# Mamba, attention and MoE decoder on one core: one product for B and C, the router's steps and the two streams' self-attention steps in another order, attention outputs copied by ScalarE

## The chip, the cores and the metric

The kernel runs on one core of a Trainium2 chip (trn2). The metric is the device time of one execution in microseconds (us); lower is better. Times are the median of 3 runs; the profile is of one more execution.

## What is computed

Eight sequences (batches) of 256 tokens, 256 channels, all in float32, pass through two layers. After every block stands a layer norm of input plus block.

```python
# layer 0: mamba without recurrence
xc    = silu(conv4(x @ W_in[:512].T));  z = x @ W_in[512:].T
proj  = xc @ W_xproj.T                       # 16 columns B, 16 columns C, 512 columns delta
bc    = (proj[..., :16] * proj[..., 16:32]).sum(-1)
x     = ln(x + ((softplus(proj[..., 32:]) * xc * bc[..., None] + D * xc) * silu(z)) @ W_out.T)
x     = ln(x + cross_attention(x, ctx_768))  # 16 heads of 64, 77 keys
# mixture: shared expert of 1024, and 2 of 8 routed experts of 256
scores = sigmoid(x @ router_w.T);  top2(scores + expert_bias)
x     = ln(x + shared(x) + routed(x, gates))
# layer 1
x     = ln(x + self_attention(x))            # 16 heads of 16, rotary embedding
x     = ln(x + cross_attention(x, ctx_768))
# last block: every token attends to the tokens of its own class (similarity over or under 0.9)
x     = ln(x + masked_attention(x))          # 16 heads of 16
```

## The kernel before

**Streams.** Even batches belong to stream 0, odd ones to stream 1. Each stream has four PSUM banks of its own (2048 float32 columns, the tile names `ps0` and `ps1`) and rooms of its own in SBUF (`m30` and `m31` are the two streams' large rooms in layer 1, `r..` the rooms for split operands, `sm..` small ones). Every product of float32 data outside the attentions is made of three matmuls on split operands (L114, L115, L116). Transposes are L644, and a plain copy by ScalarE is L1188.

**Order of the work.** Every engine works through its instructions in order. For each stage and engine the program holds the list of steps of stream 0 and that of stream 1, and a table of numbers (FIRST for layer 0, SECOND for self attention, cross attention and the projections of the last block in layer 1, LAST for the masked attention) says after how many steps of stream 0 the next step of stream 1 is issued:

```python
for j in range(4 * n):
    want = n * (j // n) + after[j % n]
    while done < want:
        next(first, None)
        done += 1
    next(second, None)
```

**Stages.** Layer 0 for all batches; then the router's scores (transposed, `rt`), gates and choice; the shared expert in four units of 256 hidden columns, two halves each, in which the streams take turns (`moe`); the indices of the tokens' places among the experts (`slots`), scatters by GpSimd with these indices, 23 routed tiles of 256 tokens, gathers back; then layer 1 for four pairs of batches, and the masked attention for four pairs.

**Router and shared expert.** DVE makes the gates of two groups of four token tiles, `gates((0, 1))`, before the shared expert and `gates((2, 3))` and `choose()` behind the first turn of stream 0. A turn of a half is: up products h1 and h2 on PE, ScalarE's silu, DVE's product (`L1509 ps<-m,ps 128x1024`) and split (`L1509 r<-ps,r`), then a turn later the down product and its sum to `xres` (`L1509 xres<-ps,xres x4`). The PE part of the indices (`slots_of`, L853 and L859) stands in stream 1's second turn, and `slots()`, one block of 27 DVE rows from L1739 to L1785, ahead of stream 1's first sum to `xres`.

**Self attention, masked attention.** A batch has four groups c of four heads. First come maxima: 16 matmuls of queries by keys fill all four banks of the stream (`mx`, L989), a DVE reduce takes the row maxima (`nm`, L1520 from 128x2048), and the next group follows. The maxima are transposed (`t2`) and added to the queries (`T2`). Then come rounds: scores with keys as rows into all four banks (`s`, L1008, 16 matmuls), Exp by ScalarE to the room (`e`, L1406, 128x2048), values times weights into bank c (`o`, L1014, 16 matmuls), and a copy of that bank's 256 columns to SBUF (`ot`, L1885 in `out_of`, by DVE), for which `s` of the next group waits. After the fourth come transposes (`t3`), the division, `oT` and the output projection `y`. In the trace a name like `m<-ps` is without stream numbers.

## Time and profile before

| | |
|---|---|
| median of 3 runs | 1649.91 us (1648.32 to 1650.14) |
| profiled execution, its own time | 1653.7 us |
| its span, first to last instruction | 1651.9 us |
| granted TensorE clock over the span | 0.921 of full |
| PE busy | 1408.8 us (85%), 12280 matmuls |
| DVE busy | 981.9 us (59%), 1739 instructions |
| ScalarE (ACT) busy | 635.9 us (38%), 743 instructions |
| GpSimd (POOL) busy | 420.0 us (25%), 434 instructions |

Stages by the trace: layer 0 to about 457 us; router and shared expert to about 640; routed experts to 769; layer 1 to 1355, a pair of batches each 143 us; the choice of classes to 1361; the masked attention to the end, a pair each 68 us.

How to read it: busy shares are over the whole span, and stages differ. A view in windows gives each engine's busy time and, as PEclk, the share of the full clock that TensorE was granted. A timeline row has start and duration in us, engine, line, operation, output<-inputs, shapes, a count, and in brackets how long the engine was idle before and who released it. A row of several matmuls (x16) is one run of them.

### The profile page before, as it was taken

How to read it: one execution, taken by the hardware profiler on the slowest of the kernel's cores; microseconds unless marked ns; L12 is line 12 of the kernel's file. 1: busy time of each engine (PE TensorE's matmuls, PEld its weight loads, DVE VectorE, ACT ScalarE, POOL GpSimd, SP SyncE). 2: the span in 40 equal slices, each digit the busy share in tenths (PEclk: the TensorE clock that was granted, in tenths of full speed). 3: DMA queues.
4: the chain of work that ended last, by engine and by line, in shares of the span. 5: the costliest groups of instructions: out<-in, count | busy, mean ns of one | idle time of the engine just before them, and what ended most of it. 6: DMA issues, size and time to landing. Idle time of an engine off the chain costs nothing.

```text
span 1651.9 us, 28489 instructions
## 1 busy us (share of the span) xinstructions
PE 1408.8 (85%) x12280; PEld 1149.8 (70%) x12280; DVE 981.9 (59%) x1739; ACT 635.9 (38%) x743; POOL 420.0 (25%) x434
## 2 busy tenths in 40 slices
PE   5899999999967999998699779969978957878785
PEld 5688888887846878997478548847855845556453
DVE  5676666756636445666745755675583555565663
ACT  3453344444522334662244244324424511422413
POOL 2230020210321653665113602622240340000000
PEclk8899999999978999998799999979999986977969
DMA  9100000000040222782000100100000020101000
GB/s 376 55 1 1 1 1 1 1 1 1 1 178 10 80 90 99 271 279 99 13 1 1 64 1 1 41 25 1 1 39 1 1 115 1 40 21 46 1 14 14
DMA packets 28495, 82.24 MB, mean 50 GB/s; under 512 B 3153, under 2 KB 13009, under 8 KB 27345
## 3 DMA queue, kind: packets, MB, share of 16 engines
q1 hardware_dynamic: 25296, 72.02, 12.1%
q0 software_dynamic: 3072, 8.39, 1.6%
q8 instruction: 97, 1.59, 0.4%
q14 instruction: 30, 0.24, 0.0%
HBM read 53.92 MB, written 26.48 MB: 49 GB/s over the span
## 4 chain that ended last, share of the span: by engine, by line
PE 33%; DVE 14%; ACT 3%; POOL 2%; issue 2%; DMA 0%; another core or an unknown queue 0%; POOLq 0%; DVEq 0%; ACTq 0%
DVE sm L1520 7%; PE ps L644 5%; PE ps L1008 4%; PE ps L1014 4%; PE ps L114 3%; PE ps L115 3%; PE ps L116 3%; PE ps L989 2%; PE ps L760 2%; PE ps L776 2%; PE ps L656 2%; PE ps L649 2%; DVE m L1509 2%; ACT m L1188 2%; DVE m L1885 1%
## 5 line engine op out<-in xcount | busy, mean ns | idle before, releaser
L1188 ACT ACTIVATE m<-ps 77x1024 f32<-77x1024 f32 (+4 forms) x248 | 183.8, 759 | 364.1 <-PE ps L116 156.8
L1520 DVE TENSOR_REDUCE sm<-ps 128x8 f32<-128x2048 f32 (+1 forms) x128 | 194.1, 1536 | 63.9 <-PE ps L989 43.6
L1509 DVE TENSOR_TENSOR r<-ps,r 128x512 fp32r<-128x512 f32 (+1 forms) x159 | 116.1, 741 | 157.0 <-ACT r L1188 157.0
L2113 POOL TENSOR_SCALAR sm<-sm 128x2 f32<-128x2 f32 x40 | 8.7, 218 | 761.9 <-DVE sm L1538 761.9
L1188 ACT ACTIVATE r<-ps 128x512 fp32r<-128x512 f32 (+1 forms) x159 | 100.7, 639 | 255.5 <-PE ps L644 120.5
L1406 ACT ACTIVATE m<-ps 128x2048 f32<-128x2048 f32 x64 | 119.3, 1877 | 154.1 <-PE ps L1008 154.1
L644 PE MATMUL ps<-cst,m 128*77 128x128 f32 (+2 forms) x1024 | 142.6, 282 | 26.7 <-DVE m L1509 6.5
L644 PEld LDWEIGHTS ps<-cst,m 128*77 128x77 f32 (+2 forms) x1024 | 117.0, 149 | 58.3 <-issue 18.0
L114 PE MATMUL ps<-r,w0h 128*128 128x256 f32 x448 | 133.0, 297 | 16.9 <-DVE r L1509 12.6
L989 PE MATMUL ps<-m 32*128 32x256 f32 x1024 | 102.5, 538 | 39.4 <-DVE sm L1520 24.0
L116 PE MATMUL ps<-r,w0l 128*128 128x256 f32 x448 | 129.8, 290 | 0.0
L115 PE MATMUL ps<-r,w0h 128*128 128x256 f32 x448 | 129.6, 289 | 0.0
L2142 POOL TENSOR_TENSOR m<-m,sm 128x616 f32<-128x616 f32 x64 | 76.7, 1216 | 147.2 <-DVE sm L1634 147.2
L989 PEld LDWEIGHTS ps<-m 32*128 32x128 f32 x1024 | 64.7, 258 | 69.1 <-DVE sm L1520 44.2
L1008 PE MATMUL ps<-m 32*128 32x256 f32 x1024 | 83.0, 448 | 31.2 <-DVE m L1885 28.7
L114 PEld LDWEIGHTS ps<-r,w0h 128*128 128x128 f32 x448 | 89.0, 199 | 19.4 <-DVE r L1509 14.7
L114 PE MATMUL ps<-w1h,r 128*128 128x256 f32 (+1 forms) x288 | 95.0, 330 | 6.3 <-DVE r L1509 6.3
L1008 PEld LDWEIGHTS ps<-m 32*128 32x128 f32 x1024 | 53.8, 211 | 61.5 <-DVE m L1885 51.1
L1885 DVE COPY m<-ps 128x256 f32<-128x256 f32 x64 | 27.0, 422 | 110.3 <-PE ps L1014 110.3
L1509 DVE TENSOR_TENSOR xres<-ps,xres 128x256 f32<-128x256 f32 (+1 forms) x104 | 50.2, 522 | 67.0 <-PE ps L116 63.7
L115 PEld LDWEIGHTS ps<-r,w0h 128*128 128x128 f32 x448 | 88.8, 198 | 1.0 <-issue 1.0
L115 PE MATMUL ps<-w1l,r 128*128 128x256 f32 (+1 forms) x288 | 89.3, 310 | 0.0
(241 smaller groups left out, 3621.1 us busy)
## 6 DMA issues: line engine op xcount, KB each, us to landing
raw<-wu_dram SPq DMA_DIRECT2D x20, 768.0 KB
keep_dram<-m SPq DMA_DIRECT2D x8, 768.0 KB, 3.2
m<-keep_dram SPq DMA_DIRECT2D x8, 768.0 KB, 4.4
xs_dram<-small SPq DMA_DIRECT2D x2, 2944.0 KB, 32.5
ys_dram<-m SPq DMA_DIRECT2D x23, 256.0 KB
room<-wu_dram SPq DMA_DIRECT2D x7, 768.0 KB, 4.7
rt<-xs_dram SPq DMA_DIRECT2D x16, 256.0 KB, 3.6
w1raw<-w_dram SPq DMA_DIRECT2D x1, 3840.0 KB, 14.4
```

What stands on the lines that cost most here:

```text
L114: pe.matmul(o, l[0], r[0], start=start, stop=False)
L115: pe.matmul(o, l[0], r[1], start=False, stop=False)
L116: return pe.matmul(o, l[1], r[0], start=False, stop=stop)
L644: return pe.transpose(o, i, ident[0:n, 0:n])
L989: m = pe.matmul(bank(st, a)[:, 256 * j:256 * j + 256], v.qT[r:r + 32, c, 128 * j:128 * j + 128], v.kT[r:r + 32, c, :], start=True, stop=True)
L1008: m = pe.matmul(bank(st, a)[:, 256 * k:256 * k + 256], v.kT[r:r + 32, c, 128 * k:128 * k + 128], v.qT[r:r + 32, c, :], start=True, stop=True)
L1014: m = pe.matmul(bank(st, c)[32 * a:32 * a + 32, 0:256], v.va[:, k, 4 * c + a, :], w[:, a, k, :], start=k == 0, stop=k == 1)
L1188: return act.activation(o, i, ACT.Copy)
L1406: act.activation(v.P, st.ps[:, :], ACT.Exp, scale=0.25).then_inc(sig.up(b, f"e{c}"), 1)
L1509: return dve.tensor_tensor(o, a, b_, op)
L1520: return dve.tensor_reduce(o, i, AX.X, op, **kw)
L2142: pool.tensor_tensor(pw, pw, v.rc[u].unsqueeze(2).to_broadcast([P, 8, CK]), ALU.mult).then_inc(sig.up(b, f"p{u}"), 1)
```

## The change

1. **B and C.** The weight W_xproj is laid out with 16 columns of zeros between B and C, so that one product of 48 columns gives B in PSUM rows 0 to 15 and C in rows 32 to 47. Before, two products of 128 columns each gave them in rows 0 to 15 of two column ranges. 12 matmuls in place of 24 per batch.
2. **Router, gates, indices.** The scores' transposes are issued in the middle of stream 0's first turn; all four groups of gates and the choice stand ahead of the shared expert's halves; `slots_of` is issued at the end of stream 1's first turn, in bank 1 of stream 0, and so waits for stream 0's silu; the wait for the copy `cp` stands on PE ahead of stream 0's first down product; the DVE block `slots()` is cut in three pieces with turns' work between them.
3. **Gathers and first norms.** Stream 1's first gather is issued one tile later; the first layer norms of layer 1 are issued between the last routed tiles.
4. **Copies `ot`.** In self attention and masked attention ScalarE copies the four outputs, 64 copies in all; DVE has none.
5. **Orders.** New tables SECOND and LAST for all engines. FIRST is unchanged.

The diff, cut:

```diff
-LAY0 = [("win", 1024), ("wz", 1024), ("wxp", 2176), ("wout", 1024), ("wq", 2048), ("wo", 2048)]
+LAY0 = [("win", 1024), ("wz", 1024), ("wxp", 2240), ("wout", 1024), ("wq", 2048), ("wo", 2048)]
...
 SECOND = {
-    "PE": [1, 2, 4, 5, 5, 6, 7, 8, 9, 10, 12, 12, 14, 14, 16, 16, 18, 19, 25, 26, 26, 26, 27, 31, 34, 35, 38, 38, 38, 41, 42, 46, 46, 48, 50, 51, 52, 52, 53, 54, 54, 54, 54, 55, 55, 56, 56, 56, 56, 56, 56, 56, 57, 57, 57, 57, 58, 60, 60],
+    "PE": [3, 5, 7, 8, 9, 10, 12, 13, 14, 15, 16, 17, 18, 19, 21, 23, 24, 25, 26, 26, 26, 26, 31, 31, 33, 35, 38, 39, 41, 43, 43, 45, 45, 47, 51, 51, 54, 56, 56, 56, 56, 56, 57, 57, 59, 59, 59, 59, 59, 60, 60, 60, 60, 60, 60, 60, 61, 61, 61],
...
+        EXPOT = [f"{w}{c}" for c in G4 for w in ("e", "ot")]
-        A1ACT = ["xT", "va", "Tk", "Tq", *EXP, "oT"]
-        A1DVE = ["xT", "c", "a0", "t0", "a1", "t1", *NM, "T2", *[f"ot{c}" for c in G4], "rc", "on", "oT", *LN]
+        A1ACT = ["xT", "va", "Tk", "Tq", *EXPOT, "oT"]
+        A1DVE = ["xT", "c", "a0", "t0", "a1", "t1", *NM, "T2", "rc", "on", "oT", *LN]
...
-                        mm3(pe, st.ps[:, 1024 + c * 256:1280 + c * 256], cols(v.wxp, A, k, slice(32 + c * 128, 160 + c * 128)), cols(v.xr, A, k), k == 0, k == 3)
-                yield
-                for c in range(2):
-                    for k in range(4):
-                        m = mm3(pe, st.ps[:, c * 256:(c + 1) * 256], cols(v.wxp, A, k, slice(16 * c, 16 * c + 128)), cols(v.xr, A, k), k == 0, k == 3)
+                        mm3(pe, st.ps[:, 1024 + c * 256:1280 + c * 256], cols(v.wxp, A, k, slice(48 + c * 128, 176 + c * 128)), cols(v.xr, A, k), k == 0, k == 3)
+                yield
+                for k in range(4):
+                    m = mm3(pe, st.ps[0:48, 0:256], cols(v.wxp, A, k, slice(0, 48)), cols(v.xr, A, k), k == 0, k == 3)
...
-                o = bank(streams[1], 3)
+                o = bank(streams[0], 1)
                 og = o[:, 0:128].rearrange("p (g i e) -> p g i e", g=4, i=4)
                 cg = chosen.rearrange("p (g i e) -> p g i e", g=4, i=4)
+                pe.wait_ge(*streams[0].moe_act.at(*MOE[0], "silu"))
                 pe.wait_ge(*gate_dve.at("four"))
...
                 for turn, (n, k) in enumerate(MOE):
                     half = st.i + 2 * k
+                    if turn == 1 and st.i == 0:
+                        pe.wait_ge(*gate_dve.at("cp"))
                     if prev is not None:
                         down(st, *prev)
-                    if turn == 1 and st.i == 1:
-                        slots_of()
                     a, b_ = turn % 2, 1 - turn % 2
                     up = tuple(k2(w[:, 0:1024]) for w in uw[n % 2])
...
-                        elif c == 1 and turn == 1 and st.i == 1:
-                            pe.wait_ge(*gate_dve.at("cp"))
                         elif c >= 2 and turn == 0:
                             pe.wait_ge(*gate_act.at("th", 2 * st.i + c % 2))
+                            if c == 2 and st.i == 0:
+                                turn_scores()
                             if c == 3 and st.i == 1:
...
-                    if turn == 0 and st.i == 0:
-                        turn_scores()
+                    if turn == 0 and st.i == 1:
+                        slots_of()
...
-                    pe.wait_ge(*dve_.at(b, f"ot{c - 1}" if c else "T2"))
+                    pe.wait_ge(*(act_.at(b, f"ot{c - 1}") if c else dve_.at(b, "T2")))
...
-                copy(v.Bc[0:16, :], st.ps[0:16, 0:256]).then_inc(sig.up(b, "B"), 1)
+                copy(v.Bc[0:16, :], st.ps[32:48, 0:256]).then_inc(sig.up(b, "B"), 1)
...
+                    yield
+                    act.wait_ge(*pe_.at(b, f"o{c}"))
+                    copy(v.OT[:, c, :], bank(st, c)[:, 0:256]).then_inc(sig.up(b, f"ot{c}"), 1)
...
-                tt(v.Bc[0:16, :], v.Bc[0:16, :], st.ps[0:16, 256:512], ALU.mult).then_inc(sig.up(b, "Bc"), 1)
+                tt(v.Bc[0:16, :], v.Bc[0:16, :], st.ps[0:16, 0:256], ALU.mult).then_inc(sig.up(b, "Bc"), 1)
...
-                dve.tensor_copy(counts, bank(streams[1], 3)[:, 0:136]).then_inc(sig.up("cp"), 1)
+                dve.tensor_copy(counts, bank(streams[0], 1)[:, 0:136]).then_inc(sig.up("cp"), 1)
+                yield
...
-                    if turn == 1 and st.i == 1:
-                        slots()
                     if turn:
                         down(st, turn - 1)
+                    if turn == 1:
+                        next(finding, None)
...
-                        gates((2, 3))
-                        choose()
-                    yield
-
-            gates((0, 1))
+                        next(finding)
+                    yield
+
+            gates(range(4))
+            choose()
+            finding = slots()
...
+            firsts = [norm_only(st, st.batches[0]) for st in streams]
...
                     routed_add(streams[0], 0)
+                    next(firsts[0])
                 elif j == NT - 2:
+                    next(firsts[0])
+                    next(firsts[0])
                     routed_add(streams[1], 1)
-            together([norm_only(st, st.batches[0]) for st in streams])
+                    next(firsts[1])
+            for first in firsts:
+                for _ in first:
+                    pass
...
-            def out_of(st, b, v, sig, pe_, c):
-                dve.wait_ge(*pe_.at(b, f"o{c}"))
-                dve.tensor_copy(v.OT[:, c, :], bank(st, c)[:, 0:256]).then_inc(sig.up(b, f"ot{c}"), 1)
...
-                elif j == NT - 3:
+                elif j == NT - 2:
                     gather(streams[1], 1)
...
+    wxp = a["L0_attn_W_xproj"].T
+    wxp = np.concatenate([wxp[:, 0:16], np.zeros((512, 16), np.float32), wxp[:, 16:]], 1)
```

**How instructions move on PE, self attention of batches 2 and 3.** Here `L989`/`L990` are maxima, `L1008`/`L1009` scores, `L1014`/`L1015` values by weights (lines before and after), `L644`/`L645` with `sm` the transposed maxima `t2`; `ps0<-m30` belongs to stream 0 and `ps1<-m31` to stream 1. Before:

```order
L989 MATMUL ps1<-m31 128x256 x8
L989 MATMUL ps0<-m30 128x256 x8
L989 MATMUL ps1<-m31 128x256 x8
L644 MATMUL ps0<-cst,sm0 128x128 x2
L644 MATMUL ps1<-cst,sm1 128x128 x2
L1008 MATMUL ps0<-m30 128x256 x8
L1008 MATMUL ps1<-m31 128x256 x8
L1014 MATMUL ps0<-m30 32x256 x8
L1008 MATMUL ps0<-m30 128x256 x8
L1014 MATMUL ps1<-m31 32x256 x8
L1008 MATMUL ps1<-m31 128x256 x8
```

Now:

```order
L645 MATMUL ps0<-cst,sm0 128x128 x2
L990 MATMUL ps1<-m31 128x256 x8
L1009 MATMUL ps0<-m30 128x256 x8
L990 MATMUL ps1<-m31 128x256 x8
L1015 MATMUL ps0<-m30 32x256 x8
L1009 MATMUL ps0<-m30 128x256 x8
L990 MATMUL ps1<-m31 128x256 x8
L1015 MATMUL ps0<-m30 32x256 x8
L990 MATMUL ps1<-m31 128x256 x8
L1009 MATMUL ps0<-m30 128x256 x8
L645 MATMUL ps1<-cst,sm1 128x128 x2
L1015 MATMUL ps0<-m30 32x256 x8
```

Before, the two streams take turns at maxima and then at rounds; now stream 1's maxima stand between stream 0's rounds, and its own rounds begin when stream 0's end.

**How instructions move on ScalarE, the same place.** `L1406`/`L1407` are the Exp, `L1188`/`L1189` copies. Before:

```order
L1188 ACTIVATE m31<-ps1 128x1024 x2
L1406 ACTIVATE m30<-ps0 128x2048
L1406 ACTIVATE m31<-ps1 128x2048
L1406 ACTIVATE m30<-ps0 128x2048
L1406 ACTIVATE m31<-ps1 128x2048
L1406 ACTIVATE m30<-ps0 128x2048
```

Now:

```order
L1407 ACTIVATE m30<-ps0 128x2048
L1189 ACTIVATE m30<-ps0 128x256
L1407 ACTIVATE m30<-ps0 128x2048
L1189 ACTIVATE m30<-ps0 128x256
L1407 ACTIVATE m30<-ps0 128x2048
L1189 ACTIVATE m30<-ps0 128x256
L1407 ACTIVATE m31<-ps1 128x2048
L1407 ACTIVATE m30<-ps0 128x2048
L1189 ACTIVATE m31<-ps1 128x256
L1189 ACTIVATE m30<-ps0 128x256
L1407 ACTIVATE m31<-ps1 128x2048
L1189 ACTIVATE m31<-ps1 128x256
```

Each Exp of a stream is followed by the 128x256 copy of its output; only at the handover from stream 0 to stream 1 does stream 0's last Exp stand between the first Exp and the first copy of stream 1.

**How instructions move on DVE, shared expert, first turns.** `ps0<-m20,ps0` and `r20` are stream 0's product and split, `ps1`, `r21` those of stream 1, `xres<-ps0` the sum of stream 0's down product, `L1739`/`L1743` the copy `cp` with which `slots()` begins. Before:

```order
L1520 TENSOR_REDUCE rt<-rt 128x32
L1509 TENSOR_TENSOR ps1<-m21,ps1 128x1024
L1509 TENSOR_TENSOR r21<-ps1,r21 128x1024
L1509 TENSOR_TENSOR xres<-ps0,xres 128x256 x4
L1509 TENSOR_TENSOR ps0<-m20,ps0 128x1024
L1509 TENSOR_TENSOR r20<-ps0,r20 128x1024
L1739 COPY rt<-ps1 128x136
```

Now:

```order
L1524 TENSOR_REDUCE rt<-rt 128x32
L1513 TENSOR_TENSOR ps0<-m20,ps0 128x1024
L1513 TENSOR_TENSOR r20<-ps0,r20 128x1024
L1743 COPY rt<-ps0 128x136
L1513 TENSOR_TENSOR ps1<-m21,ps1 128x1024
L1513 TENSOR_TENSOR r21<-ps1,r21 128x1024
L1513 TENSOR_TENSOR xres<-ps0,xres 128x256 x4
L1513 TENSOR_TENSOR rt<-rt,cst 128x64
```

The choice (the reduce of 32) now ends ahead of stream 0's first product and not between the two streams' first products, and the copy `cp` comes a turn earlier.

## Rows read from the trace of the kernel before

**Rows 1.** The page: granted clock of TensorE in 40 slices, tenths.

```profile
PEclk8899999999978999998799999979999986977969
```

**Rows 2.** Windows: layer 0, MoE start, maxima, rounds, cross attention, masked attention.

```profile
core 0: us, PE busy (x) PEld busy (x) DVE busy (x) ACT busy (x) POOL busy (x), PEclk, DMA share, GB/s
130.00:400.00 270.00, 251.70 (x1899) 222.64 (x1898) 175.58 (x343) 119.71 (x137) 34.06 (x44) 0.98 0.00 1
500.00:540.00 40.00, 29.81 (x154) 25.48 (x153) 24.37 (x64) 7.06 (x7) 6.89 (x7) 0.87 0.06 20
...
1078.65:1098.00 19.35, 12.46 (x124) 8.01 (x128) 17.83 (x9) 0.00 (x0) 3.29 (x4) 0.73 0.09 28
1098.00:1124.50 26.50, 20.50 (x260) 10.98 (x252) 10.62 (x31) 14.91 (x8) 2.10 (x4) 0.88 0.01 2
1124.50:1183.00 58.50, 57.43 (x428) 48.42 (x428) 33.15 (x58) 26.80 (x40) 16.43 (x18) 1.00 0.00 1
1380.00:1652.00 272.00, 210.11 (x3057) 140.24 (x3055) 157.14 (x277) 83.84 (x82) 7.45 (x16) 0.82 0.06 21
```

**Rows 3.** Chain of waits: first maxima of two pairs, layer 1 and last.

```profile
935.40 1.19 PE ps L989 x16
...
1078.65 1.19 PE ps L989 x16
...
1511.40 2.09 PE ps L989 x16
...
1579.36 2.09 PE ps L989 x16
```

**Rows 4.** Timeline of PE, start of a pair's projections and its next stage.

```profile
1050.23 0.40 PE L114 MATMUL ps<-w1h,r 128*128 128x512 f32 x1
...
1134.73 0.60 PE L644 MATMUL ps<-cst,xres 128*128 128x128 f32 x4
```

**Rows 5.** Groups by form, one pair of layer 1, 935.40 to 1078.65.

```profile
L1520 DVE TENSOR_REDUCE sm<-ps 128x8 f32<-128x2048 f32 x8 | 18.0, 2288 | 4.7 <-PE ps L989 3.0 <-remote 1.7
```

**Rows 6.** Timeline, a half round of each stream.

```profile
965.33 1.15 PE L1008 MATMUL ps<-m 32*128 32x256 f32 x16 [0.55 <-DVE m L1885]
...
966.40 1.07 PE L1014 MATMUL ps<-m 128*32 128x256 f32 x16
966.54 1.88 ACT L1406 ACTIVATE m<-ps 128x2048 f32<-128x2048 f32 x1 [0.82 <-PE ps L1008]
967.54 0.42 DVE L1885 COPY m<-ps 128x256 f32<-128x256 f32 x1 [2.27 <-PE ps L1014]
...
968.02 1.15 PE L1008 MATMUL ps<-m 32*128 32x256 f32 x16 [0.55 <-DVE m L1885]
```

**Rows 7.** Timeline of PE at the end of layer 0.

```profile
453.40 0.28 PE L114 MATMUL ps<-w0h,r 128*128 128x256 f32 x1
...
453.76 0.28 PE L114 MATMUL ps<-w0h,r 128*128 128x256 f32 x1
```

**Rows 8.** Timeline of PE, shared expert, where it waited.

```profile
505.65 0.39 PE L114 MATMUL ps<-uw,r 128*128 128x256 f32 x1 [2.58 <-DVE r L1509]
...
515.06 0.50 PE L114 MATMUL ps<-xTall,uw 128*128 128x512 f32 x1 [2.02 <-DVE xres L1509]
...
531.77 0.80 PE L114 MATMUL ps<-xTall,uw 128*128 128x512 f32 x1 [5.58 <-DVE xres L1509]
```

**Rows 9.** Timelines of DVE and POOL: first and last index step, last scatter.

```profile
523.38 0.30 DVE L1739 COPY rt<-ps 128x136 f32<-128x136 f32 x1 [1.68 <-PE ps L859]
...
530.22 0.18 DVE L1785 CAST sm<-sm 128x32 uint32<-128x32 f32 x1
...
600.14 0.96 POOL L2186 DMA_INDIRECT xs_dram<-w1f,sm  x1 [0.30 <-issue]
```

**Rows 10.** Groups by form, 400 to 1652 us: ScalarE's copies from PSUM.

```profile
L1188 ACT ACTIVATE m<-ps 128x1024 f32<-128x1024 f32 x44 | 44.0, 1021 | 62.1 <-PE ps L116 41.4 <-PE ps L644 16.4 <-issue 4.2
...
L1188 ACT ACTIVATE m<-ps 128x512 f32<-128x512 f32 x48 | 26.9, 600 | 90.7 <-PE ps L644 45.0 <-PE ps L116 40.9 <-POOL m L2261 4.7
```

More of the change, by code:

```diff
@@ L291, in ffn_dve @@
                 o += [(b, s) for s in ("nx0", "nx", "x2", *NM, "T2")]
-                o += [nxt[0], (b, "ot0"), nxt[1], (b, "ot1"), nxt[2], (b, "ot2"), nxt[3], nxt[4]]
-                o += [(b, s) for s in ("ot3", "xr", "xn", "xc", "rc", "on", "ov", "oT", *LN)]
+                o += nxt
+                o += [(b, s) for s in ("xr", "xn", "xc", "rc", "on", "ov", "oT", *LN)]
             return [s for s in o if s is not None]
@@ L311, in ffn_act @@
                     o += [(b, s) for s in ("Tqa", "Tk", "Tq", "xe")]
-                o += [(b, s) for s in ("ex", "xo", *EXP)]
+                o += [(b, s) for s in ("ex", "xo", *EXPOT)]
                 nxt = [(b + 2, s) for s in ("Tqa", "Tk", "Tq", "xe")] if b + 2 < B else []
@@ L1064, in a1 @@
                 yield
-                pe.wait_ge(*dve_.at(b, "ot3"))
+                pe.wait_ge(*act_.at(b, "ot3"))
                 turn_out(st, b, v, sig)
@@ L1143, in fa @@
                 yield
-                pe.wait_ge(*dve_.at(b, "ot3"))
+                pe.wait_ge(*act_.at(b, "ot3"))
                 turn_out(st, b, v, sig)
@@ L1935, in a1 @@
                 yield
-                for c in range(4):
-                    yield
-                    out_of(st, b, v, sig, pe_, c)
                 yield
@@ L2066, in fa @@
                 nxt = front(st, b + 2) if b + 2 < B else iter(())
-                for c in range(4):
+                for c in range(5):
                     next(nxt, None)
-                    yield
-                    out_of(st, b, v, sig, pe_, c)
                     yield
@@ L2224, in norm_only @@
                 yield
-            together([norm_only(st, st.batches[0]) for st in streams])
+            for st in streams:
+                for _ in norm_only(st, st.batches[0]):
+                    pass
             last_moe(pool)
@@ L2356, in kv @@
         return np.concatenate([wk[0:P], wv[0:P], np.concatenate([wk[P:CD], wv[P:CD]], 0)], 1)
+    wxp = a["L0_attn_W_xproj"].T
+    wxp = np.concatenate([wxp[:, 0:16], np.zeros((512, 16), np.float32), wxp[:, 16:]], 1)
     conv = np.concatenate([a["L0_attn_conv_w"], a["L0_attn_conv_b"][:, None], a["L0_attn_D"][:, None]], 1)
-    w0 = np.concatenate([rows(a["L0_attn_W_in"][:512].T), rows(a["L0_attn_W_in"][512:].T), rows(a["L0_attn_W_xproj"].T), rows(a["L0_attn_W_out"].T),
+    w0 = np.concatenate([rows(a["L0_attn_W_in"][:512].T), rows(a["L0_attn_W_in"][512:].T), rows(wxp), rows(a["L0_attn_W_out"].T),
                          rows(a["L0_xattn_Wq"]), rows(a["L0_xattn_Wo"])], 1)
```

12 lines of the change are left out of this document (6 added, 6 removed).

## The prediction

> **What bounds the kernel now.** I read the page first, then the chain of waits for the stages, then the stages in windows, then timelines where the change touches them. Granted clock by slice [rows 1] is full or nearly full in layer 0 and around the middle, and lowest (6 to 7 tenths) in slices of the masked attention. The windows [rows 2] show two kinds of stage. In layer 0 PE is busy 251.7 of 270 us, in layer 1's cross attention 57.43 of 58.5: there only fewer matmuls help. In the self attention no engine is full. With the maxima DVE is the bound, 17.83 of 19.35 us, and PE, 12.46, is granted 0.73 of its clock. In the rounds PE has 20.50 of 26.5, ScalarE 14.91, DVE 10.62, and the masked attention is alike: PE 210 of 272 us at 0.82. So the stages that the new tables touch are bound by handoffs, and the two phases have opposite bounds. A pair of batches takes 1078.65 - 935.40 = 143.25 us in layer 1 and 1579.36 - 1511.40 = 67.96 in the masked attention [rows 3]. I cost the change part by part; it has five parts with a price.
>
> **B and C.** Three split matmuls of 256 columns take 453.76 - 453.40 = 0.36 us [rows 7], 0.12 each; 12 fewer per batch are 1.43, in eight batches 11.4 us. PE works 93% of the stage [rows 2], so nearly all of it lies on the path; but the products stand in a stretch where DVE's conv and ScalarE's steps of the same batch follow one another, and I take 85%: **9.7** (bounds 7 and 11.4). The copy from rows 32 to 47 is the same ScalarE instruction. I cost a product of 48 output rows as one of 128, since no row shows one of 48.
>
> **Router, gates, indices.** PE waits 2.58, 2.02 and 5.58 us before three products [rows 8]: for the split behind the second pair of gate groups, for a sum behind it, and for stream 1's sum, which stands behind the whole index block, 523.38 to 530.40 on DVE [rows 9]. In the change all gates stand ahead of the first product while PE has the halves' products to do, and the block is in three pieces under products. Laid out by hand with the rows' durations: the choice is done at about 504.0 (509.6 before), stream 0's first down product starts at 507.7, the counts at 518, the last index at 524.7, and the product that stood at 540.30 starts at 527.5. That is 12.8 less: about 10.2 of gaps become 2.8 (the new waits: the first product for its two DVE steps, the down product for `cp`), and 3 to 5 come from products that ran slow behind the gaps; the window from 500 to 540 had 0.87 of the clock [rows 2]. Behind PE's new wait for `cp` stands all of PE's stream 0; DVE reaches `cp` 0.3 us behind the split, so it costs little. I take **12** (bounds 5.7, the index time alone, and 13). Scatters start 5.7 earlier; the last was at 600.14 [rows 9], and the first routed tile is some 40 us behind it, so GpSimd's queue is no bound either way.
>
> **Gathers and first norms.** One gather a tile later, norms ahead of the last tile's output: **1** (0 to 3); DVE had the norms to do directly behind.
>
> **Self attention.** From the first projection of a pair to the transposes ahead of its cross attention the trace has 1134.73 - 1050.23 = 84.5 us [rows 4]. In it lie 8 maxima at 2.29 on DVE, 18.3 us [rows 5], and 8 half rounds at 968.02 - 965.33 = 2.69, 21.5 us [rows 6]: both streams pay for each other's steps, 39.8 together. In the new order a stream goes alone: a maximum is 1.19 of PE [rows 3] plus 0.1 plus 2.29, so 3.58, four are 14.3. A round is 1.21 from `s` to the Exp, 1.88 of Exp, 0.05, 1.14 from `o` to its copy [rows 6], the copy and 0.06. ScalarE's copies from PSUM take 1.02 us at 1024 columns and 0.60 at 512 [rows 10], by a straight line 0.39 at 256, against DVE's 0.42 [rows 6]; so a round is 4.73, take 4.8, four 19.2. Stream 1's maxima stand beside stream 0's rounds (DVE is free there), its rounds beside what stream 0 does next. With all steps laid out (only stream 0's projection and rotary steps now stand ahead of the first maximum) 84.5 becomes 76.5, **8.0** less. Given back: the next pair's gathers and norms now meet the division on DVE, 1.6, and stream 1's last transposes stand ahead of stream 0's cross attention, 1.0; 5.4 stay. The clock takes more: stream 1's rounds, alone, keep PE busy 2.2 of 4.8 us, less than the 12.46 of 19.35 that ran at 0.73 [rows 2]. A group of 16 matmuls is 1.19 at the full level and 2.09 at the half level [rows 3], 0.90 more; five such groups on the path are 4.5, and 0.9 would stay. The maxima before were at 0.73 as well and now run beside other products, so I take the middle, 3.5 a pair; four pairs less 1 at the end, where stream 1 is late: **13** (2.6 to 20.6). The move of the copies alone is worth nothing here, 0.03 us each.
>
> The row says ScalarE has room, 14.91 of 26.5, but DVE with 10.62 has more [rows 2]. The Trainium skill (Perfetto Trace Analysis, Optimizing Scalar/DVE Operations) says that work should go from DVE to ScalarE if DVE is saturated. By that rule part 4 brings nothing, and without the orders' gain the sum would end near 1627; what I count comes from the orders, which let DVE do maxima in the rounds: without its four copies (1.7) and with four maxima (9.2) it would be some 18 of 26 us busy there.
>
> **Masked attention.** The same 39.8 become 14.3 + 19.2 = 33.5, 6.3 less of 67.96, and 0.7 more since DVE's projections for the next pair no longer wait between copies: 61.0 a pair at equal clock. Here the clock was low before, 0.82 over the stage [rows 2], and `L989` at 2.09 [rows 3]; four more slow groups, 3.6, would leave about 3. I take 5, three periods, less 1.3 at the end: **13.7** (7.7 to 19.7).
>
> **Sum.** 9.7 + 12 + 1 + 13 + 13.7 = 49.4. The profiled execution took 1653.7 (span 1651.9); that gives 1604.3, and against the median of 1649.91, which lies 3.8 below it, 1600.5. Forecast **1601**. All lower bounds together give 23, so 1627; all upper ones 68, so 1582.
>
> **Rivals.**
> - *The clock.* If TensorE is at its 1.2 GHz level in all of a lone stream's rounds, eight groups at 0.90 are 7.2 a pair: layer 1 loses 1.8 a pair and 7 in all, the masked attention gains nothing. 9.7 + 12 + 1 - 7 - 1 = 14.7: about 1635. For it: 0.73 and 0.82 in sparse stretches [rows 2]. Against it: in the half rounds before, PE was 77% busy and `L1008` at full speed [rows 6], and stream 0's rounds now have maxima beside them. The Trainium skill (TensorE: Matmul & The Clock Gate, A second HAM failure mode) tells of a kernel whose short idles between groups made the clock swing between the levels, which speaks for this rival; the trace agrees in that 1.19 and 2.09 both occur for the same 16 matmuls. Chance 0.15.
> - *Only the index time.* If the slow products behind the gaps stay slow, the MoE term is 5.7: 1607, and 1611 if the routed stage waits for POOL. Against it: no gap of over 2.6 us is left in my layout. Chance 0.08; inside the range.
> - *Copies behind the other stream's Exp: slower.* ScalarE works in order. If a stream's copy regularly stands behind the other's Exp, `s` waits for it: a half step is then 1.88 + 0.39 + 0.06 + 1.22 = 3.55 in place of 2.69, 0.86 for each of 64 copies, 55 us, and the attention gains are lost too: 1649.9 - 22.7 + 55 = 1682. It decides from 22.7 / 0.86 = 26 of 64 copies on. For it: the Exps of both streams did follow each other in the old order. Against it: in the new order of ScalarE one copy of eight per pair of layer 1 (stream 1's first) stands behind the other stream's Exp, and none in the masked attention. Chance 0.07.
> - *Nothing comes of it,* as the gains are all taken back by later waits: 1650. Both the PE-bound layer 0 and the gaps speak against it. Chance 0.03.
> - *More,* near 1580: the clock rises as maxima and rounds fill one another's gaps. Chance 0.05.
>
> **How the numbers follow.** The forecast case has 0.62. A difference of 0.2%, 3.3 us, is about what a measurement of this kernel can tell from no change. Faster by more: 0.62 + 0.15 + 0.08 + 0.05 = 0.90; same 0.03; slower 0.07. The range 1580 to 1630 holds the bounds of the sum and leaves out the slower case, the unchanged one and more than half of the clock's.
>
> **What would show it.** Layer 0 ends near 447 in place of 457, with 96 matmuls fewer. In the shared expert no PE gap over 2.6 us, and the last index 5 to 6 us earlier. In layer 1 the first maxima of two pairs 139 to 140 us apart, the copy of 128x256 on ScalarE at 0.39, DVE over 60% busy in the rounds; in the masked attention 62 to 64 apart. `L1009` or `L1015` groups at 2 us in most of a lone stream's rounds would show the clock's rival; an idle time of `L1009` released by a ScalarE copy of well over 0.6 would show the slower one. I am wrong if a pair of layer 1 takes over 143, or if the shared expert's end moves by less than 5 us.

## The result, and the profile after

The changed kernel took 1636.99 us in the median of 6 runs (1630.64 to 1641.26), the kernel before 1650.03 beside it (6 runs): ratio 0.9922, interval 0.9899 to 0.9944. It is faster by 13 us, and I forecast 49, in a range that ended at 1630. A later set of runs gave 0.9954 (0.9935 to 0.9972) for the same kernel.

The stages in windows, of the kernel before. A window ends with the last product on layer 0's weights, with the first transpose of layer 1's input on PE, with the reload of the masked attention's data behind the choice of classes, and with the span; columns as in [rows 2]. By the first mark layer 0 ends at 462.7 us, not at about 457 as I had put it:

```profile
0.00:462.70 462.70, 414.54 (x3087) 364.71 (x3088) 297.05 (x547) 202.70 (x231) 83.45 (x90) 0.97 0.11 39
462.70:769.20 306.50, 269.75 (x1786) 243.16 (x1786) 171.25 (x309) 125.14 (x151) 139.93 (x82) 0.95 0.42 146
769.20:1356.60 587.40, 499.60 (x4208) 390.18 (x4208) 347.30 (x571) 220.87 (x273) 189.15 (x246) 0.93 0.06 21
1356.60:1651.90 295.30, 224.88 (x3202) 151.75 (x3202) 166.32 (x313) 87.16 (x88) 7.45 (x16) 0.79 0.07 25
```

The same four of the changed kernel:

```profile
0.00:450.20 450.20, 400.50 (x2992) 350.42 (x2992) 297.69 (x547) 203.77 (x231) 83.54 (x90) 0.97 0.11 40
450.20:741.40 291.20, 265.13 (x1785) 239.74 (x1784) 171.78 (x309) 124.73 (x151) 140.36 (x82) 0.96 0.45 152
741.40:1334.50 593.10, 492.70 (x4208) 387.09 (x4208) 336.64 (x541) 230.05 (x305) 190.93 (x246) 0.96 0.06 21
1334.50:1633.80 299.30, 216.23 (x3202) 149.46 (x3202) 155.39 (x280) 99.25 (x120) 7.45 (x16) 0.83 0.08 24
```

Layer 0 is 12.5 us shorter, router to routed experts 15.3, and then the picture turns: layer 1 is 5.7 **longer** and the masked attention 4.0 longer, at a higher TensorE clock in both (0.93 to 0.96, 0.79 to 0.83). Subtract PE's busy time from each window and the two attentions say the same: PE is busy 6.9 and 8.7 us less (its clock), and idle 100.4 in place of 87.8 and 83.1 in place of 70.4, so 12.6 and 12.7 us more.

The shared expert went as laid out. Timelines of PE and DVE in the changed kernel:

```profile
496.64 0.58 PE L114 MATMUL ps<-uw,r 128*128 128x256 f32 x1 [0.97 <-DVE rt L1743]
```

```profile
496.29 0.29 DVE L1743 COPY rt<-ps 128x136 f32<-128x136 f32 x1
...
514.93 0.18 DVE L1791 CAST sm<-sm 128x32 uint32<-128x32 f32 x1
```

The wait for `cp` costs 0.97 us. Behind it the products of both streams follow each other without a gap to beyond 527 us, where PE before had waited 2.58, 2.02 and 5.58 us [rows 8]. The last index comes 15.3 us earlier than at 530.22 [rows 9]. Of these, 11.2 were there when the shared expert's first product started (479.46 against 490.69), and 4.1 are the index work's own; I had laid out 5.5.

The self attention of the third pair on PE. Which stream a row belongs to follows from the tables, which fix PE's order. In the kernel before, the first maximum of stream 0 and its last product of values by weights are

```profile
1073.82 1.15 PE L989 MATMUL ps<-m 32*128 32x256 f32 x16
...
1120.63 1.07 PE L1014 MATMUL ps<-m 128*32 128x256 f32 x16
```

(the row at 1078.65 of [rows 3] is stream 1's first maximum, and 1050.23 of [rows 4] stream 0's projection for the last block, the last step of the batch before). In the changed kernel, from that same projection of stream 0 on:

```profile
1010.60 0.50 PE L114 MATMUL ps<-w1h,r 128*128 128x512 f32 x1 [0.46 <-DVE r L1513]
...
1041.75 1.15 PE L990 MATMUL ps<-m 32*128 32x256 f32 x16 [1.81 <-ACT m L1189]
...
1050.94 1.15 PE L990 MATMUL ps<-m 32*128 32x256 f32 x16 [2.60 <-DVE sm L1524]
1055.26 2.09 PE L990 MATMUL ps<-m 32*128 32x256 f32 x16 [1.51 <-DVE sm L1524]
1059.77 0.44 PE L645 MATMUL ps<-cst,sm 128*128 128x128 f32 x2 [0.20 <-DVE sm L1524]
...
1081.67 1.07 PE L1015 MATMUL ps<-m 128*32 128x256 f32 x16 [0.70 <-ACT m L1407]
...
1091.77 1.07 PE L1015 MATMUL ps<-m 128*32 128x256 f32 x16
1093.35 1.15 PE L1009 MATMUL ps<-m 32*128 32x256 f32 x16 [0.50 <-ACT m L1189]
...
1098.05 1.07 PE L1015 MATMUL ps<-m 128*32 128x256 f32 x16
1099.05 2.03 PE L657 MATMUL ps<-ctxT,w1f 128*128 128x98 f32 x16
...
1101.79 0.60 PE L645 MATMUL ps<-cst,xres 128*128 128x128 f32 x4
```

The row at 1081.67 is stream 0's last product of values by weights; 1091.77, 1093.35 and 1098.05 are stream 1's last rounds, and 1099.05 keys of stream 0.

On DVE the first row maximum of pairs 2 to 4 of layer 1 and of the masked attention (`L1524`), with the last step of the norm (`L1518`) ahead of stream 0's cross attention:

```profile
899.24 2.29 DVE L1524 TENSOR_REDUCE sm<-ps 128x8 f32<-128x2048 f32 x1 [0.51 <-PE ps L990]
...
1043.03 2.29 DVE L1524 TENSOR_REDUCE sm<-ps 128x8 f32<-128x2048 f32 x1 [0.56 <-PE ps L990]
...
1094.71 1.50 DVE L1518 TENSOR_SCALAR xres<-xres,sm 128x256 f32<-128x256 f32 x2 [1.14 <-POOL sm L2122]
...
1185.70 2.29 DVE L1524 TENSOR_REDUCE sm<-ps 128x8 f32<-128x2048 f32 x1 [0.56 <-PE ps L990]
...
1429.73 2.29 DVE L1524 TENSOR_REDUCE sm<-ps 128x8 f32<-128x2048 f32 x1 [4.43 <-PE ps L990]
...
1494.28 2.29 DVE L1524 TENSOR_REDUCE sm<-ps 128x8 f32<-128x2048 f32 x1 [2.97 <-PE ps L990]
...
1559.11 2.29 DVE L1524 TENSOR_REDUCE sm<-ps 128x8 f32<-128x2048 f32 x1 [4.27 <-PE ps L990]
```

Pairs of layer 1 follow each other at 140.4 (the first, from 758.84), 143.8 and 142.7 us, before at 143.3, 143.2 and 143.2: 2.8 us in three periods, and nothing after the first. In the masked attention the second and third periods are 64.6 and 64.8 in place of 68.0, 3.3 less each, and the first is 75.3 in place of 67.9. And there is a price at the end of each stage. GpSimd's step of the choice, one row per stream, in the changed kernel, and below it the chain of the kernel before, where both stand in one row of two:

```profile
1305.61 5.82 POOL L2301 TENSOR_TENSOR sm<-sm,cst 128x32 f32<-128x32 f32 x1 [7.24 <-DVE sm L1513]
...
1327.55 5.82 POOL L2301 TENSOR_TENSOR sm<-sm,cst 128x32 f32<-128x32 f32 x1 [3.95 <-DVE sm L1513]
```

```profile
1344.66 10.78 POOL sm L2293 x2
```

Stream 1 ends layer 1 22 us behind stream 0, before 5.4. From the last pair's first maximum to stream 1's choice step it is now 1327.5 - 1185.7 = 141.8 us; the same stretch was 130.9 before (1219.1 to 1350.0). Some 2 to 3 us of the difference only mean that the first maximum now stands earlier in its pair: in the first pair it comes 17.5 us into layer 1, before 20.2.

### The profile page after: what moved, and what is told of

Read it like the earlier page. It is cut to its first block, busy times and chain, and to the rows that moved or that the text cites. A ratio compares the mean times of both kernels' runs of the same rounds, so it can differ in the third digit from the quotient of the medians.

```text
span 1633.8 us, 28300 instructions
## 1 busy us (share of the span) xinstructions
PE 1374.6 (84%) x12184; PEld 1126.7 (69%) x12184; DVE 961.5 (59%) x1675; ACT 657.8 (40%) x807; POOL 422.3 (26%) x434
## 3 DMA queue, kind: packets, MB, share of 16 engines
q1 hardware_dynamic: 25296, 72.05, 12.5%
## 4 chain that ended last, share of the span: by engine, by line
PE 63%; DVE 22%; ACT 9%; issue 4%; POOL 1%; DMA 1%; another core or an unknown queue 0%; SPq 0%; POOLq 0%; DVEq 0%; ACTq 0%
PE ps L114 12%; PE ps L116 11%; PE ps L115 11%; DVE sm L1524 8%; PE ps L645 5%; PE ps L990 4%; DVE m L1513 4%; PE ps L650 3%; PE ps L1015 3%; ACT m L1189 3%; PE ps L657 3%; ACT m L1407 3%; PE ps L1009 3%; PE ps L776 2%; PE ps L760 2%
## 5 line engine op out<-in xcount | busy, mean ns | idle before, releaser
L1189 ACT ACTIVATE m<-ps 77x1024 f32<-77x1024 f32 (+7 forms) x312 | 205.7, 681 | 447.4 <-PE ps L116 192.6
L1524 DVE TENSOR_REDUCE sm<-ps 128x8 f32<-128x2048 f32 (+1 forms) x128 | 196.8, 1537 | 115.2 <-PE ps L990 91.4
L1189 ACT ACTIVATE r<-ps 128x512 fp32r<-128x512 f32 (+1 forms) x159 | 100.1, 639 | 229.7 <-PE ps L645 103.8
L645 PE MATMUL ps<-cst,m 128*77 128x128 f32 (+1 forms) x1024 | 149.0, 290 | 26.0 <-DVE m L2067 7.4
L645 PEld LDWEIGHTS ps<-cst,m 128*77 128x77 f32 (+1 forms) x1024 | 122.7, 153 | 58.8 <-issue 19.6
L1407 ACT ACTIVATE m<-ps 128x2048 f32<-128x2048 f32 x64 | 119.7, 1877 | 81.0 <-PE ps L1009 81.0
L114 PE MATMUL ps<-r,w0h 128*128 128x256 f32 (+1 forms) x416 | 124.0, 298 | 17.1 <-DVE r L1513 12.8
L990 PE MATMUL ps<-m 32*128 32x256 f32 x1024 | 84.5, 450 | 51.0 <-DVE sm L1524 40.6
L115 PE MATMUL ps<-r,w0h 128*128 128x256 f32 (+1 forms) x416 | 120.6, 290 | 0.0
L116 PE MATMUL ps<-r,w0l 128*128 128x256 f32 (+1 forms) x416 | 120.2, 289 | 0.0
L2148 POOL TENSOR_TENSOR m<-m,sm 128x616 f32<-128x616 f32 x64 | 76.5, 1216 | 150.9 <-DVE sm L1638 150.9
L990 PEld LDWEIGHTS ps<-m 32*128 32x128 f32 x1024 | 52.3, 209 | 76.0 <-DVE sm L1524 56.4
L114 PE MATMUL ps<-w1h,r 128*128 128x256 f32 (+1 forms) x288 | 96.3, 334 | 9.3 <-DVE r L1513 9.3
L1015 PE MATMUL ps<-m 128*32 128x256 f32 x1024 | 72.1, 400 | 28.5 <-ACT m L1407 28.5
L114 PEld LDWEIGHTS ps<-r,w0h 128*128 128x128 f32 (+1 forms) x416 | 80.3, 193 | 19.5 <-DVE r L1513 14.8
L116 PE MATMUL ps<-w1h,r 128*128 128x256 f32 (+1 forms) x288 | 90.7, 315 | 0.0
L1009 PE MATMUL ps<-m 32*128 32x256 f32 x1024 | 74.4, 408 | 12.0 <-ACT m L1189 10.6
L760 PE MATMUL ps<-m 128*128 128x154 f32 x512 | 79.3, 301 | 3.0 <-DVE m L1513 2.3
```

The lines of the kernel that those rows point to most:

```text
L114: pe.matmul(o, l[0], r[0], start=start, stop=False)
L115: pe.matmul(o, l[0], r[1], start=False, stop=False)
L116: return pe.matmul(o, l[1], r[0], start=False, stop=stop)
L645: return pe.transpose(o, i, ident[0:n, 0:n])
L760: m = pe.matmul(bank(st, 2 * j + n // 2)[:, 154 * (n % 2):154 * (n % 2) + 154], v.QT[:, 4 * i + n, j * 128:(j + 1) * 128], v.K[:, 4 * i + ...
L990: m = pe.matmul(bank(st, a)[:, 256 * j:256 * j + 256], v.qT[r:r + 32, c, 128 * j:128 * j + 128], v.kT[r:r + 32, c, :], start=True, stop=True)
```

## The experiments

My theory after the first comparison: the front parts (products, router, indices) give what was forecast, and both new attention orders lose. The main rival was that the attentions' loss comes from what stands ahead of them or from the clock, and would be there with the old orders too. The first set takes the parts one by one. Each kernel is the kernel before with these parts of the change:

```diff
 l0_only:      + one product for B and C
 moe_only:     + router, gates, indices, gathers, first norms
 front_only:   + both of these
 front_second: + both, + self attention new (SECOND, copies by ScalarE)
```

**l0_only.**

> The kernel before with the one product for B and C alone. Theory (parts add up, and each stage's end in the two traces tells its part): layer 0 ended 12.6 us earlier in the changed kernel (462.7 to 450.2), and nothing behind it changes, so 1650.0 - 12.6 = 1637. Rival (the product is worth its 12 matmuls at 0.12 us, 85% of them on the path, and the rest of the 12.6 came from elsewhere): 1640.3. Third: most of the product was hidden beside DVE's steps, 1645 or more.

1642.18 us, ratio 0.9971 (0.9953 to 0.999) to the kernel before: 4.8 us, interval 1.6 to 7.7. In its trace layer 0 ends at 451.5, 11.2 earlier. The time on the chip is nearest to the rival's 1640; that all of the trace's 11 us reach the end is not shown.

**moe_only.**

> The kernel before with the parts on router, gates, indices, gathers and first norms alone. Theory: from the end of layer 0 to the first self attention the changed kernel is 15.2 us shorter, so 1634.8. Rival (only the indices' 5.7 us count, the rest of the difference is the clock's, at other places in another run): 1644.

1637.97 us, ratio 0.9944 (0.9919 to 0.997): 9.2 us, between theory and rival. The stage took 290.3 us in the trace, where l0_only, with this part as before, took 300.9 and the kernel before 306.5: a gain of 10.6 to 16. Single traces of the same instructions differ by 5 us here.

**front_only.**

> Both front parts, with both attentions as before: old tables SECOND and LAST, copies by DVE. Theory (the new attention orders cost 5.3 us in layer 1 and 4.1 in the masked attention): 1650.0 - 27.8 = 1622, faster than the changed kernel by 15 less 0 to 5 (9.4 by the traces). Rival (the attentions' loss is made by what stands ahead of them, such as the time at which weights and gathers land, and would come with the old orders too): 1637, as the changed kernel.

1628.43 us, 0.99 (0.9862 to 0.9937). The changed kernel had 0.9922 (0.9899 to 0.9944), so these ratios alone don't tell the two apart; the third set does, and there the rival falls. It is 6 us over the theory, and its trace says where: the masked attention, the same instructions in the same order, took 303.3 us against 295.3 before, at a clock of 0.75 against 0.79:

```profile
1323.70:1627.00 303.30, 236.71 (x3202) 160.11 (x3202) 166.30 (x313) 87.28 (x88) 7.45 (x16) 0.75 0.07 24
```

PE's idle time there is 66.6 us, before 70.4; its busy time is 11.8 more, for the same 3202 matmuls: that is the clock.

**front_second.**

> As front_only, with the new order and ScalarE copies in the self attention of layer 1 alone; the masked attention as before. Theory (a pair gains 0.9 us, three periods, and the stream that now runs 22 us late costs 10.9 at the stage's end): 5.3 over front_only, so 1627.5, and the two choice steps on GpSimd some 22 us apart. Rival (layer 1's order is a gain, and only the masked attention loses): under front_only by 3 us or more.

1632.55 us, 0.9917 (0.9882 to 0.9952). The interval overlaps that of front_only. But layer 1 takes 594.2 us in the trace (front_only 585.0), and the choice steps lie 23 us apart, as the theory has it; the theory's sum for the whole kernel, 1627.5, is 5 us short.

The second set asks for the masked attention, for the copies' engine, and for the clock.

```diff
 front_last:     front_only + masked attention new (LAST, copies by ScalarE)
 old_orders_act: front_only + copies by ScalarE, old PE order; ScalarE:
-    e0(A) e0(B) e1(A) e1(B) ...
+    e0(A) e0(B) ot0(A) e1(A) ot0(B) e1(B) ot1(A) ...
 last_new_dve:   front_last with DVE's copies, DVE's order:
+    T2(A) ot0(A) nm0(B) nm1(B) ot1(A) nm2(B) ot2(A) nm3(B) T2(B) ot3(A)
 double_mx:      front_only, in maxima_of of PE:
-    for j in range(2):
+    for j in (0, 1, 0, 1):
```

(A and B are stream 0 and 1.)

**front_last.**

> As front_only, with the new order and ScalarE copies in the masked attention alone; layer 1 as before. In the changed kernel the stage took 299.3 us with 105 us of low clock; in front_only it took 303.3 with 153 (in the kernel before 295.3 with 121). Theory (the new order itself costs about 8 us for the late stream, and the higher clock that it brings gives 12 back): the stage takes 297 to 301 with less low clock than 153, layer 1 takes 585, total 1622 to 1627, same or slightly faster than front_only. Rival (the order is a plain loss of 4, as the first comparison of traces has it): 1632.

1635.42 us beside a kernel before of 1655.55: 0.9863 (0.9809 to 0.9917). The stage took 301.9 us. It isn't told apart from front_only (0.99 in the first set). The time itself is above theory and rival, but so is the kernel before above its 1647.94 of the first set.

**old_orders_act.**

> Both front parts and the ScalarE copies, but the old orders of both attentions, so that each copy of one stream stands behind the Exp of the other on ScalarE. The rival of the prediction's slower side priced this at 0.86 us for each of 64 copies: 55 over front_only, so 1683, with half rounds of 3.55 us in place of 2.69. Theory 2 (the copies of ScalarE fit in the waits that are there): within 5 us of front_only, 1628.

1649.3 us, 0.9958 (0.9932 to 0.9985), slower than front_only by some 10 us by the ratios and 20 by the two traces, and not by 55. The mechanism was there in full. Its half rounds, in the timeline of the self attention (`L1013`, `L1019`, `L1411` and `L1193` are `s`, `o`, Exp and copy in this kernel):

```profile
1080.43 1.88 ACT L1411 ACTIVATE m<-ps 128x2048 f32<-128x2048 f32 x1 [1.26 <-PE ps L1013]
1082.21 0.38 ACT L1193 ACTIVATE m<-ps 128x256 f32<-128x256 f32 x1
...
1082.64 1.15 PE L1013 MATMUL ps<-m 32*128 32x256 f32 x16 [1.27 <-ACT m L1193]
...
1083.85 1.88 ACT L1411 ACTIVATE m<-ps 128x2048 f32<-128x2048 f32 x1 [1.26 <-PE ps L1013]
```

A half round is 1083.85 - 1080.43 = 3.42 us, against 2.69 [rows 6] and a forecast of 3.55. But there are six of them a pair and not eight, and in layer 1 the old first rounds had waited longer: the second Exp of stream 0 came 5.3 us behind stream 1's first (1068.0 to 1073.3 in front_only), now 3.4 (1073.6 to 1077.0); DVE's first copy had stood behind the next pair's norm in its order. From first to last Exp the pair's rounds take 22.3 us, in front_only 21.4. Layer 1 grew by 11.5 us, the masked attention by 8.2.

**last_new_dve.**

> As front_last, with the four copies on DVE between stream 1's maxima. Theory (the copies' engine is worth nothing, the order is all): within 3 us of front_last. Rival (a copy waits up to 2.29 us behind a maximum on DVE, so the new order needs ScalarE): 16 copies of stream 0, 1 us each, so front_last + 10 to 16.

1639.56 us, 0.9922 (0.9887 to 0.9958); front_last had 0.9863 (0.9809 to 0.9917). The intervals overlap, the medians differ by 4 us where theory had 3 at most, and the stages took 301.2 and 301.9 us. So in this order DVE could have kept the copies; by the traces the 4 us between the medians lie ahead of the stage. The same was not tried in the self attention, where the new order and ScalarE's copies were only run together.

**double_mx.**

> front_only, with the 16 matmuls of each group of maxima issued twice (same result), in both attentions; the second time lies beside the other stream's DVE reduce of 2.29 us. Theory (the low TensorE clock of the sparse maxima costs time later, about 0.25 us for each us of it, by front_only's and before's masked attention, 153 and 121 us low, 303.3 and 295.3 long): low-clock time in the masked attention falls under 110 and the stage gains 5 or more, partly eaten by 1.07 for the first maximum of a pair: 1620 to 1628. Rival (the clock follows, but does not pay): slower by 8 x 1.07 to 32 x 1.07, 1637 to 1662.

1643.3 us, 0.9922 (0.9895 to 0.9948). The masked attention in windows:

```profile
1339.20:1639.20 300.00, 232.23 (x3714) 167.75 (x3714) 166.07 (x313) 87.26 (x88) 7.45 (x16) 0.89 0.07 24
```

With 512 matmuls more the clock went from 0.75 to 0.89, and the stage from 303.3 to 300.0, which is within the spread of its times in other traces (295.3 to 303.3). Layer 1, where the clock had less to give (0.93 in front_only, 0.95 here), took 599.4, 14 more. So the clock followed PE's activity, and that it pays is not shown: at best it paid for the matmuls that raised it. The whole execution in the trace is 12 us longer than front_only's (1639.2 against 1627.0), and the median lies in the rival's range.

The third set is two by two on one chip, five rounds each: each attention in its old and its new form.

**front_only_b.**

> The same kernel as front_only, again, on one chip with the other three of this set (two by two: each attention in its old or its new form). Theory (one time cost of the late stream, 9 to 11 us in layer 1, against no gain per pair there; in the masked attention cost and clock's gain nearly equal): front_only_b is faster than the changed kernel by 6 to 12 us. Rival (the attentions' part of the change is even): within 3 us of it.

**front_second_b.**

> The same kernel as front_second: only the self attention new. Theory: layer 1's stage takes 592 to 596 us against 585 to 588, so 5 to 9 over front_only_b. Rival: even with it.

**front_last_b.**

> The same kernel as front_last: only the masked attention new. Theory: within 4 us of front_only_b, on either side, as the stage took 301.9 and 303.3, and the fastest or second fastest of the four. Rival: it gains by 5 or more, since pairs follow at 64 to 66 us in place of 68 to 69.

**both_again.**

> The changed kernel again, on the same chip. Theory: slowest of the four or even with front_second_b, 6 to 12 over front_only_b; the sum of the two single steps within 3 us. Rival (the two new orders need each other, since stream 1 comes late out of layer 1): faster than front_second_b and front_last_b.

| kernel | median us | ratio to before (interval) | layer 1 | masked attention |
|---|---|---|---|---|
| before | 1647.46 | | | |
| front_only_b | 1625.25 | 0.9848 (0.9815 to 0.9882) | 585.0 | 300.8 |
| front_last_b | 1628.93 | 0.9874 (0.9842 to 0.9907) | 589.4 | 298.5 |
| front_second_b | 1634.13 | 0.9917 (0.9887 to 0.9947) | 593.2 | 297.6 |
| both_again | 1640.89 | 0.9954 (0.9935 to 0.9972) | 597.4 | 303.3 |

By the medians the new self attention costs 8.9 us alone and 12.0 beside the new masked attention; that is clear of the intervals. The new masked attention costs 3.7 alone and 6.8 beside the new self attention, and both times the intervals overlap; its stage took 2.3 us less in the one pair of traces and 5.7 more in the other. A small loss is likely there and not shown; shown is that the forecast gain of 13.7 did not come. Both together cost 15.6, more than the 6 to 12 that I expected of them. front_only, the change without its new attention orders and copies, has the lowest median, 15.6 us under the changed kernel and 22.2 under the kernel before. The windows of front_only_b for layer 1 and the masked attention, to be held against those of the changed kernel above, and its choice steps, in one row of two again:

```profile
737.60:1322.60 585.00, 498.46 (x4208) 389.23 (x4208) 347.09 (x571) 221.10 (x273) 188.89 (x246) 0.94 0.06 22
1322.60:1623.40 300.80, 229.67 (x3202) 156.21 (x3202) 166.02 (x313) 87.20 (x88) 7.45 (x16) 0.77 0.08 24
```

```profile
1310.67 10.83 POOL L2306 TENSOR_TENSOR sm<-sm,cst 128x32 f32<-128x32 f32 x2
```

PE's idle time tells the orders apart without the clock. In the masked attention it is 66.6 to 71.1 us in the eight traces with the old order and 83.1 to 84.4 in the four with the new one and its copies on ScalarE (after, front_last, front_last_b, both_again): the order costs 12 us or more of idle time, and PE's shorter busy time, 214 to 220 us against 225 to 237, gives most of it back or all. In layer 1 it is 84 to 89 in the old order and 97 to 101 in the new one. In the trace of front_last_b layer 1, which its change does not touch, is 4.4 us longer than in front_only_b, more than the 3.7 between the medians.

One question was left: does the late stream cost only in its lone tail, which a last pair in the old order would avoid, or did stream 0 gain nothing by running ahead? Two kernels take the new orders for three pairs and the old one for the fourth:

```diff
 mixed_tail (on front_second), mixed_last (on front_last):
-        want = n * (j // n) + after[j % n]
+        want = n * (j // n) + after[j // n][j % n]      # after = [new] * 3 + [old]
```

**mixed_tail.**

> front_second (self attention new, masked attention old), but the last of the four pairs of layer 1 in the old order, copies still on ScalarE. Theory (the late stream is no cost of its tail alone: stream 1's work has to be done after stream 0's in whatever order, and stream 0 has gained nothing by then, 426.9 to 430.7 for three periods against 427.8 and 428.1): the old order makes stream 0 wait for stream 1 in the last pair, so the stage keeps at least half of its loss, 589 to 595 us, total 1629 to 1635. Rival (the loss sits in stream 1's lone tail, which lockstep avoids): the stage takes 585 and the two choice steps lie 5.5 us apart, total 1625 or less.

1638.49 us, 0.9958 (0.9932 to 0.9985). Layer 1:

```profile
739.00:1335.50 596.50, 490.39 (x4208) 385.56 (x4208) 336.63 (x541) 230.12 (x305) 189.44 (x246) 0.96 0.06 21
```

The choice steps do lie 5.4 us apart, but the stage takes 596.5. The step from the third pair to the last is 153.9 us in place of 143: what stream 0 had been ahead is lost again in it. The rival falls; stage and median are a little above the theory's range too.

**mixed_last.**

> front_last (only the masked attention new), with its last pair in the old order. Theory: as the theory of mixed_tail, the stage takes 297 to 302 us as with the new order in all four pairs. Rival (three pairs at 65 us and a tail of 70 in place of 75): 293 to 295, total 1620 to 1624, and the best kernel of all.

1639.71 us, 0.9943 (0.9927 to 0.9958). The stage takes 311.7 us, 13 more than front_last_b, in an execution that was 10 us longer than this kernel's median (1649.64), so up to 10 of the 13 may be that execution's own. Still its ratio is worse than that of front_last_b, on another chip and clear of the intervals: the rival falls, and whether the theory's 297 to 302 us hold for the stage stays open. In both stages going back to the old order for the last pair did not win the loss back.

## Why the prediction was wrong

**B and C: right in the stage.** 9.7 forecast; the trace has 11 to 12.5, so all of the product's 11.4 are on the path there. The whole kernel moved by 4.8 (1.6 to 7.7) in l0_only, half of the 9.7; where the rest went is not shown.

**Router, gates, indices: right.** 12 and 1 forecast for this and the routed end; 15.3 by the profiled executions, 10.6 against l0_only's trace, 9.2 on the chip. PE's waits went, no wait of over 1.3 us took their place around the indices. All front parts together were forecast at 22.7, and the medians of front_only_b and the kernel before differ by 22.2; the first set gave the same kernel 0.99, some 16 us, so the close match is partly luck.

**Self attention: the step that failed.** 13 forecast as gain, 8.9 measured as loss (front_second_b against front_only_b). Stream 0 in the third pair, by PE's rows:

| from ... to ... | before, us | changed, us |
|---|---|---|
| projection for the last block, first maximum | 23.6 | 31.2 |
| first maximum, end of the last values by weights | 47.9 | 41.0 |
| from there to the transposes ahead of cross attention | 13.0 | 19.1 |
| these transposes, next projection for the last block | 59.0 | 53.0 |
| in all | 143.5 | 144.2 |

The prediction's arithmetic for stream 0 alone holds: from its first maximum to the end of its last product of values by weights it takes 41.0 us (1041.75 to 1082.74), before 47.9 (1073.82 to 1121.70), so 6.9 less where 39.8 - 33.5 = 6.3 was forecast. The failure is "its rounds beside what stream 0 does next", which I had charged with 1.0. From there to the transposes ahead of stream 0's cross attention it is 19.1 us (to 1101.79), before 13.0 (to 1134.73): DVE had that input ready at 1096.2, and on PE, which takes its steps in order, keys, values and stream 1's last rounds stood ahead of it for another 5.6 us, before for 1.2. PE is 92% busy in this stretch (before 94%), so stream 1's rounds don't hide there: they add, and 6.0 of the 6.9 are gone.

The second half of the step is at the start of the pair. I had laid out that "only stream 0's projection and rotary steps now stand ahead of the first maximum". But stream 1, now late, still has the output projection of its cross attention and its projection for the last block to do, and they stand there on PE: from stream 0's projection to its first maximum it is 31.2 us (1010.60 to 1041.75), before 23.6 (1050.23 to 1073.82). So the stretch of 84.5 us that was to become 76.5 became 91.2. Stream 0's cross attention, which has less of stream 1 beside it, is shorter by 5.9 for it and the period stays where it was. Layer 1 has the same 4208 matmuls in either order, and there was little idle time in the cross attention (PE 98% busy [rows 2]) to put the late stream's steps into. The clock had a small share: `L990` of 2.09 at 1055.26 is one such group. There is a slip of size as well: the middle of 0.9 and 5.4 is 3.15 and not 3.5, which alone makes the 13 some 11.6.

**The end of a stage: mis-sized.** I charged 1 and 1.3 us for the late stream. From the last pair's first maximum to the choice it is 141.8 - 130.9 = 10.9 us more in layer 1 (141.8 and 140.1 in both_again and front_second), since the choice needs both streams; less what the earlier first maximum and the first period gave, layer 1 as a whole is 8.1 us longer than in front_only_b (593.1 against 585.0). In the masked attention the last pair's first maximum to the end is 1633.8 - 1559.1 = 74.7 against 70.3. Lockstep has one loose end of 5 us, the shifted order one of 22. With four pairs a stage, 3.3 us a pair in the masked attention cannot pay for a start and an end.

**Masked attention.** 13.7 forecast, none came: front_last_b's median is 3.7 over front_only_b's, within the intervals. The period's gain, 3.3, was near the lower bound I gave (3); the first period, which I had let gain 5 like the others, is 75.3 us, and the tail, put at 1.3, is 4.4 longer. Part of the first is not the order's: with the front parts and the old order the first period is 71.6 (front_only_b) and no longer 67.9, at a clock of 0.81 in place of 0.85 and nearly the same idle time of PE (13.7 and 13.0 us). In the new order that idle time is 20.3.

**The clock's rival** gave the time almost exactly (1635), for the wrong reason. I had the clock fall in the lone rounds. It rose: 0.96 and 0.83 in place of 0.93 and 0.79, and in stream 0's rounds it was full. The Trainium skill (TensorE: Matmul & The Clock Gate, A second HAM failure mode) tells of a clock that swings between its two levels where matmul groups have short idles between them; the trace agrees in that the same 16 matmuls take 1.15 and 2.09 us, and the clock has a mean of 0.75 to 0.79 in the masked attention in the old order and 0.82 to 0.83 in the new one. Which order is faster doesn't follow from it. **The slower rival** had its half round right (3.42 for 3.55), its count wrong, and its condition wasn't met. The Trainium skill (Perfetto Trace Analysis, Optimizing Scalar/DVE Operations) says that offloading work from DVE to ScalarE may make sense if DVE is saturated. DVE was not, and the trace agrees that the copies' engine is worth nothing: last_new_dve and front_last took 301.2 and 301.9 us for the masked attention. For the self attention no run shows it.

## What to carry to other kernels

Two streams in lockstep look wasteful where a phase is bound by one engine, but here a shift between them only moved the late stream's steps to places where PE was busy already. It can pay only if what the two then do side by side has different bounds for the whole of the period; lay out the second stream to the first one's next full stage, and charge the lateness once at every point that needs both. Undo the parts of a change one by one even if the sum is a gain: here half the edits gave 22 us and the other half took back 15. And read idle and busy time of the bound engine apart, since a higher clock can hide a worse order.

## What the hardware showed that I had not expected

The same instructions in the same order, the masked attention of the kernel before, took 295.3 to 303.3 us in eight traces of six kernels that differ only ahead of it, with TensorE's clock at 0.75 to 0.79 of full. PE's idle time was 66.6 to 71.1 us: the spread of 8 us is in its busy time. Two executions of one kernel, front_only and front_only_b, gave 303.3 and 300.8. So a gain ahead of a stage in which the clock is at its lower level for part of the time reached the end short by up to 8 of 28 us, and a difference of under some 8 us between two kernels can't be given to a stage by one trace.
